# A Mamba layer in rounds: eight states scaled by ScalarE and folded by one accumulating transfer, softplus in one transfer fewer, the output's last passes a round later

## What is computed

```
xv    = silu(conv(x @ W_in) + conv_b)
ssm   = xv @ W_x;  dt_raw, Bp, Cp = split(ssm, (RDT, 16, 16))
delta = softplus(dt_raw @ W_dt + b_dt)
dA    = exp(delta[..., None] * A)
dBx   = delta[..., None] * Bp[:, :, None, :] * xv[..., None]
h     = scan(h -> dA * h + dBx)                  # along the sequence of 512
y     = einsum('bldn,bln->bld', h, Cp) + xv * D  # 16 states n
out   = y @ W_out
```

## Time and profile before

| | |
|---|---|
| median of 3 runs | 754.86 us (753.48 to 755.99) |
| the profiled execution's own time | 754.58 us |
| its span, first to last instruction | 752.7 us |
| busy: PE, DVE, ACT, POOL | 665.7, 645.0, 501.6, 490.3 us |
| mean granted clock of PE | 0.988 |
| from one state-1 add of DVE to that of the next round (549.21 to 602.28) | 53.07 us |

### The profile page before, as it was taken

One profiled execution on the slowest core, in us unless ns is written; L12 is line 12 of the kernel. 1 busy time (PEld: TensorE's weight loads), 2 busy tenths in 40 slices (PEclk: granted clock), 3 DMA queues, 4 the chain that ended last, 5 costly groups with the idle time before them and its releaser, 6 DMA issues. The chain is left out here.

```text
span 752.7 us, 12948 instructions
## 1 busy us (share of the span) xinstructions
PE 665.7 (88%) x4001; PEld 491.8 (65%) x4001; DVE 645.0 (86%) x1102; ACT 501.6 (67%) x1020; POOL 490.3 (65%) x305
## 2 busy tenths in 40 slices
PE   1898999999799998768998998998999999988785
PEld 0885555655565553446876787787777777768765
DVE  5878877777567656989999999999999999999997
ACT  1565666666444444879879778788788797796463
POOL 1001663000055445086999999999999999999995
PEclk9999999999999999989999999999999999999999
DMA  7900110001222217534424336237046156254000
GB/s 203 294 1 7 39 40 28 0 0 28 60 64 68 71 48 98 169 147 127 108 99 128 98 113 144 69 113 182 30 150 151 38 158 154 76 130 120 1 15 16
DMA packets 43050, 67.43 MB, mean 90 GB/s; under 512 B 6264, under 2 KB 30208, under 8 KB 42992
## 3 DMA queue, kind: packets, MB, share of 16 engines
q1 hardware_dynamic: 31744, 48.35, 20.4%
q0 software_dynamic: 9520, 17.78, 11.6%
q10 hardware_dynamic: 1728, 0.57, 0.3%
HBM read 46.01 MB, written 9.67 MB: 74 GB/s over the span
## 5 line engine op out<-in xcount | busy, mean ns | idle before, releaser
L1710 DVE TENSOR_TENSOR_SCAN xnT_all<-psum,nfT_all 128x1024 f32<-128x1024 f32 x128 | 288.5, 2275 | 0.1
L1260 PEld LDWEIGHTS psum<-W_out,xnT_all 128*128 128x128 f32 x2048 | 237.3, 193 | 56.9 <-issue 54.2
L1260 PE MATMUL psum<-W_out,xnT_all 128*128 128x128 f32 x2048 | 242.7, 277 | 29.5 <-DVE acc L1726 27.3
L1433 ACT ACTIVATE psum<-delta,A 128x511 f32<-128x511 f32 x256 | 165.0, 683 | 59.8 <-DVE xnT_all L1710 59.7
L1240 POOL TENSOR_TENSOR nfT_all<-nf_rows,du 128x1024 f32<-128x1024 f32 x63 | 147.2, 2361 | 23.0 <-DVE nfT_all L1792 22.5
L1240 POOL TENSOR_TENSOR nfT_all<-attn_all,du 128x1024 f32<-128x1024 f32 x64 | 157.4, 2601 | 1.1 <-DVE xnT_all L1710 1.1
L571 POOL DMA_INDIRECT moe_dram<-xnT_all x39 | 37.6, 963 | 119.9 <-ACT xnT_all L827 119.9
L1726 DVE SCALAR_TENSOR_TENSOR acc<-psum,Cc,acc 128x128 f32<-128x128 f32 x284 | 77.9, 338 | 6.1 <-PE psum L1260 6.1
L560 POOL DMA_INDIRECT xs_dram<-nf_rows,pos x32 | 33.1, 1036 | 76.3 <-DVE pos L881 57.3
L1260 PE MATMUL psum<-vo_all,W_taps 128*128 128x512 f32 (+3 forms) x128 | 58.7, 606 | 0.7 <-ACT vo_all L1465 0.7
L1484 ACT ACTIVATE ts<-psum,Cc 128x128 f32<-128x128 f32 x188 | 52.8, 360 | 4.1 <-PE psum L1260 4.1
(11 more groups left out here) (218 smaller groups left out, 1128.0 us busy)
## 6 DMA issues: line engine op xcount, KB each, us to landing
nf_rows<-bt_dram SPq DMA_DIRECT2D x32, 512.0 KB, 4.7
attn_all<-bt_dram SPq DMA_DIRECT2D x32, 512.0 KB, 3.9
delta<-rl POOLq DMA_DIRECT2D x7, 512.0 KB, 7.0
e<-ab POOLq DMA_DIRECT2D x7, 512.0 KB, 5.8
delta<-e POOLq DMA_DIRECT2D x7, 512.0 KB, 6.1
xs_dram<-attn_all SPq DMA_DIRECT2D x4, 645.0 KB, 8.3
xnT_all<-xs_dram SPq DMA_DIRECT2D x39, 64.5 KB, 1.9
x_all<-in_x_dram SPq DMA_DIRECT2D x8, 256.0 KB, 6.0
```

The source lines that it names most:

```text
L1260: return nc.tensor.matmul(o, l, r, start=start, stop=stop)
L1433: ins = nc.scalar.activation(dA[:, i % RA, k, 1:L], delta[:, p, h, 1:L], ACT.Exp, scale=A[:, h, 2 * q + k:2 * q + k + 1])
L1710: nc.vector.tensor_tensor_scan(hring[:, i % R, :, :].rearrange("p n l -> p (n l)"), dA[:, i % RA, :, :].rearrange("p n l -> p (n l)"), dbx ...
```

## The change

ACT scales states 8 and 14 as well, so `ON_ACT` has eight states and DVE adds eight. The scaled slices 0 to 3 (states 5, 7, 8, 9) stand in a tile `early`, slices 4 to 7 (11, 12, 14, 15) in `late`, which is a part of `res_all`. Once a round POOL issues one accumulating transfer of 128x2048 values (`fold`) that adds all of `early` onto `late`; three POOL sums then add the four slices of `late`. Two of the softplus transfers become one of 128x2x1024 values (`softplus_sums`, step 6). `output_gate` and `output_rows` of a row move from steps 5 and 7 of the next round to steps 0 and 1 of the round after it, and the store goes with them.

```diff
-        ON_ACT = (5, 7, 9, 11, 12, 15)
+        ON_ACT = (5, 7, 8, 9, 11, 12, 14, 15)
+        FOLD = len(ON_ACT) // 2
+        LAST = sum(n < NS - 2 for n in ON_ACT)
...
-            ts = sb6("ts", [P, len(ON_ACT), TPB, D])
+            early = sb6("early", [P, FOLD, TPB, D])
+            late = res_all[:, 0:FOLD * TPB, :].rearrange("p (i j) d -> p i j d", j=TPB)
...
-                            if end and q == 6:
-                                store()
+                            if b > 1 and q == 2:
+                                store(b - 2)
...
-                    def sum_scaled(c, i):
...
+                    def fold():
+
+                        pool.wait_ge(S["ts"], at(b - 1, "ts", len(ON_ACT)))
+                        alone(pool)
+                        pool.dma_start(late[:, :, :, :], early[:, :, :, :], accum_op=ALU.add).then_inc(s_sp, 16)
+
+                    def sum_folded(i):
+
+                        if i == 1:
+                            pool.wait_ge(s_sp, summed(b, 1))
+                            alone(pool)
+                            pool.wait_ge(S["os"], at(b - 2, "os", 1))
+                        else:
+                            pool.wait_ge(S["accP"], at(b - 1, "accP", i - 1))
+                        nc.gpsimd.tensor_tensor(accP[:, :, :], ts(FOLD) if i == 1 else accP[:, :, :],
+                                                ts(FOLD + i), ALU.add).then_inc(S["accP"], 1)
...
-                    def softplus_high():
+                    def softplus_sums():
                         w("lg", 1)
                         w("rl", KH)
-                        alone(pool)
-                        pool.dma_start(delta[:, 1 - p, :, :], rl[:, :, :], accum_op=ALU.add).then_inc(s_sp, 16)
-
-                    def softplus_low():
                         w("e1", 1)
                         alone(pool)
-                        pool.dma_start(e1[:, :, :], ab[:, :, :], accum_op=ALU.add).then_inc(s_sp, 16)
+                        pool.dma_start(delta_e1[:, 1 - p:3:1 + p, :, :], rl_ab[:, :, :, :], accum_op=ALU.add)\
+                            .then_inc(s_sp, 16)
...
-                            if q in (1, 2, 3) and end:
-                                sum_scaled(b - 1, q + 1)
-                            if q == 4 and end:
-                                sum_scaled(b - 1, 5)
-                                output_sum()
-                            if q == 5:
+                            if q == 0 and b > 1:
+                                output_gate(b - 2)
+                            if q == 1 and b > 1:
+                                output_rows(b - 2)
+                            if q == 3 and end:
+                                fold()
+                            if q == 5 and end:
+                                sum_folded(1)
+                                sum_folded(2)
+                            if q == 6:
                                 if prep:
-                                    softplus_high()
+                                    softplus_sums()
                                 if end:
-                                    output_gate()
-                            if q == 6 and prep:
-                                softplus_low()
+                                    for i in range(3, FOLD):
+                                        sum_folded(i)
                             if q == 7:
-                                if end:
-                                    output_rows()
                                 if prep:
                                     deltas()
-                                sum_scaled(b, 1)
+                                if end:
+                                    output_sum()
...
-                        if q == 0 and end and scan:
-                            scale_state(b - 1, 1 - p, 5)
-                        if scan and 3 <= q < 8:
-                            scale_state(b, p, q - 3)
+                        if scan:
+                            for n in (2 * q - 2, 2 * q - 1):
+                                if n in ON_ACT:
+                                    scale_state(b, p, n)
+                                elif n < 0 and n + NS in ON_ACT and end:
+                                    scale_state(b - 1, 1 - p, n + NS)
```

More of the change, by code:

```diff
@@ L1052, in attention_moe_mamba_ffn @@
             G1 = sb6("G1", [P, 2, L])
[L1053 to L1056, removed]
+            rl_ab = sb6("rl_ab", [P, 2, KH, L])
+            rl, ab = rl_ab[:, 0, :, :], rl_ab[:, 1, :, :]
+            delta_e1 = sb6("delta_e1", [P, 3, KH, L])
+            delta, e1 = delta_e1[:, 0:2, :, :], delta_e1[:, 2, :, :]
             du = sb6("du", [P, 2, KH, L])
@@ L1060, in attention_moe_mamba_ffn, with ts @@
             skip_sb = sb6("skip_sb", [P, 2, TPB, D])
-            ts = sb6("ts", [P, len(ON_ACT), TPB, D])
+            early = sb6("early", [P, FOLD, TPB, D])
+            late = res_all[:, 0:FOLD * TPB, :].rearrange("p (i j) d -> p i j d", j=TPB)
+            def ts(i):
+                return early[:, i, :, :] if i < FOLD else late[:, i - FOLD, :, :]
             accP = sb6("accP", [P, TPB, D])
@@ L1079, in xn1 @@
             def xn1(i):
-                return ts[:, i, :, :] if i < LATER else xnb[:, :, :]
+                return early[:, i, :, :] if i < LATER else xnb[:, :, :]
             names, S = names6, M
@@ L1085, in at, with summed @@
                 return (b + 2) * names[n] + c
+            def summed(b, k):
+                return 16 * (3 * b - (b > 0) + k)
             bM, Gb = (4, 5), (6, 7)
@@ L1120, in round_, with store @@
                             .then_inc(s_bst, 16)
-                    def store():
-                        sp.wait_ge(S["ow"], at(b - 1, "ow", 1))
+                    def store(c):
+                        sp.wait_ge(S["ow"], at(c, "ow", 1))
                         alone(sp)
-                        sp.dma_start(out[ds(b - 1, 1)].rearrange("a (j p) d -> p (a j) d", p=P), ow[:, :, :])\
+                        sp.dma_start(out[ds(c, 1)].rearrange("a (j p) d -> p (a j) d", p=P), ow[:, :, :])\
                             .then_inc(s_o, 16)
@@ L1136, in round_ @@
                                 .then_inc(s_bld[q], 16)
-                            if end and q == 6:
-                                store()
-                    elif end:
-                        store()
+                            if b > 1 and q == 2:
+                                store(b - 2)
+                    elif scan:
+                        store(b - 2)
+                        store(b - 1)
+                    else:
+                        store(b - 1)
                 rounds(sp, round_)
@@ L1203, in drives @@
                     def drives():
-                        pool.wait_ge(s_sp, (b + 1) * 48)
+                        pool.wait_ge(s_sp, summed(b + 1, 0))
                         alone(pool)
@@ L1244, in round_ @@
                             drives()
+                        else:
+                            output_gate(b - 1)
+                            output_rows(b - 1)
                     elif end:
-                        for i in range(2, len(ON_ACT) - 1):
-                            sum_scaled(b - 1, i)
-                        pool.wait_ge(S["accP"], at(b - 1, "accP", len(ON_ACT) - 1))
+                        for i in range(1, LAST):
+                            sum_last(i)
+                        pool.wait_ge(S["accP"], at(b - 1, "accP", LAST - 1))
                         pool.wait_ge(S["G1"], at(b - 1, "G1", 1))
@@ L1427, in decays @@
                     elif q == 0:
-                        act.wait_ge(s_sp, b * 48)
+                        act.wait_ge(s_sp, summed(b, 0))
                     for h in range(KH):
@@ L1475, in conv_silu, with scale_state @@
                         .then_inc(S["yh"], 1)
-                def scale_state(c, p, i):
-                    n = ON_ACT[i]
+                def scale_state(c, p, n):
+                    i = ON_ACT.index(n)
                     act.wait_ge(S["G"], at(c, "G", n + 1))
                     act.wait_ge(S["C"], at(c, "C", 1))
-                    act.wait_ge(S["accP"], at(c, "accP", max(i, 1) + 1 - len(ON_ACT)))
+                    if i >= FOLD:
+                        act.wait_ge(S["accP"], at(c - 1, "accP", max(i - FOLD, 1)))
+                    elif c:
+                        act.wait_ge(s_sp, summed(c, 1))
                     for j in range(TPB):
-                        ins = nc.scalar.activation(ts[:, i, j, :], bank[Gb[n % 2]][:, j * P:(j + 1) * P], ACT.Copy,
+                        ins = nc.scalar.activation(ts(i)[:, j, :], bank[Gb[n % 2]][:, j * P:(j + 1) * P], ACT.Copy,
                                                    scale=Cc[:, p, j, n:n + 1])
```

33 lines of the change are left out of this document (18 added, 15 removed).

## The result

| | before | after |
|---|---|---|
| median of 5 runs each | 755.99 us (753.48 to 757.59) | 767.16 us (761.61 to 767.70) |
| the profiled execution's own time, its span | 754.58, 752.7 us | 761.61, 759.7 us |
| a round, scan (0,0) to scan (0,0), rounds 1 to 5 | 53.07 to 53.08 us | 54.45 us each |

The changed kernel is slower: the ratio is 1.013, with a 95% interval of 1.0093 to 1.0168. The profiled execution is the shortest of its five.

The account below looks back on a forecast made before the run. The prediction took a loop through DVE and PE, 53.07 us a round, as the bound. +8.0 (state 8) + 1.3 (merged transfer) = +9.3 on 754.58 is 763.9; forecast 764.0, 762.5 to 766 at 60%, range 759.5 to 771.

Parts of the forecast that it names:

- State 8: On ACT behind the decays of step 6, it makes PE start state 10 1.33 later; six rounds, +8.0 us.
- DVE's saved adds become waits: DVE saves 1.02 each in steps 5 and 0, but mostly waits longer for PE; 0.25 + 1.02 before state 1.
- no change: Rival: ACT's scaling of state 8 does not hold PE, rounds stay at 53.07; 755.9 us, chance 8%.
- faster: Rival: DVE is the bound by itself, so removed adds of states 8 and 14 give -15.3; 739.3 us, chance 8%.
- State 14: Step 0: DVE's saved 1.02 becomes waiting in rounds 1 to 6; on ACT it costs nothing, by 0.3 us.
- the loop through state 8: DVE's state 1 add through scan (5,1), state 8's removal, then PE until the next state 1 add; 53.07 before.
- The merged transfer: Softplus transfer of doubled size lands after 8.7 (bounds 5.8 and 11.6); free in rounds 1 to 6, +1.3 with round 7.
- The cover of 2 us: In rounds 1 to 6 the merged transfer could land some 2 us later than 8.7 at no cost.
- My second rival: Transfers scale with size: merged one lands after 11.6, deciding from about 10.8; +17, 771.6 us, chance 12%.
- `fold`: Issued by POOL in step 3, lands after 8.5 to 9.7; costs nothing up to some 11.9.
- Round 7: POOL's products bind at scan (1,1), 2.4 later; scan (2,0) 2.2 later, less 0.85 of state 8: +1.3 us.
- the first rival: Merged transfer takes no longer than one before, 5.8 or less: 8.0 - 1.6 = +6.4, 761 us, chance 12%.

Follow-up runs that it names:

- x1: The kernel before with state 8 on ACT in place of state 9, nothing else changed: 763.08 us against 755.54, ratio 1.011.
- x3: The changed kernel with ACT taking state 8 out between the two halves of the decays of step 6, ahead of its wait for scan (5,1): 768.63 us, ratio 1.0189.
- x5: x3 with the softplus sums in two transfers again, the first in step 5: 755.6 us against 754.51, ratio 1.0018.
- x2: The changed kernel with state 10 on ACT instead of state 8: 769.05 us, ratio 1.0172.
- x8: The changed kernel once more, without an edit, for a second profile: 764.23 us against 754.51, ratio 1.0139.
- x6: x3 with fold moving only one slice of four, leaving out the contributions of states 7, 8 and 9: 757.27 us, ratio 1.0037.

## Why the prediction was right, step by step

**State 8: right in place and size.** PE was to start state 10 2.55 behind the scan (5,1) (1.22 + 1.33); it started 2.54 behind it. Rounds 0 to 5 were to become 8.0 longer; they became 1.01 + 5 x 1.375 = 7.9 longer. x1 shows that this part alone does it, and x3 that it is the place in ACT's list and not the work.

**DVE's saved adds become waits: right.** A wait of 1.27 was forecast at the add of state 1; it is 0.52 + 0.66, part of it already at the add of state 0. What DVE wins in step 5 was to lengthen its next wait for PE; ahead of state 13 that grew from 0.62 to 2.43. This and x1 end the rivals "no change" and "faster".

**State 14: right for rounds 1 to 5,** where the loop through state 8 is the whole round; x1, without state 14 on ACT, has the same length.

**The merged transfer: right in effect, 1.0 too long.** It landed after 7.7, not 8.7; the first two rivals needed 5.8 or less and 10.8 or more. Its time on the engines doubled as assumed (2.71 to 5.2). The base was too long: 5.8 was a median, while the very transfer whose 2.71 I used landed after 5.0, and 5.0 + 2.5 is 7.5. The Trainium skill, "DMA: Bandwidth & Descriptors", section "Anatomy of one DMA", would have it at about 4.4 (an estimate by its fit); the trace does not agree, with 7.7 here and 9.5 in x3. Its "Rules for kernel authors" say to coalesce many small transfers into one large one, and call those under 64 KB mostly overhead. The transfers here have 512 KB, and two of them, landing after 5.3 with the first 5.67 ahead, gave shorter rounds than one that the same consumer waits for entirely (x5 against x3).

**The cover of 2 us: held, but is narrower than it reads.** At rounds of 54.45, POOL waits for e1 and for the merged transfer (2.85 and 1.37 in round 4), and from round 1 to round 5 no engine shows a wait for POOL. But this is cover at the pace that state 8 sets. As soon as the loop is shortened, POOL's chain binds (x2, x3) at 53.5 to 56.7. My second rival, transfers of 11.6, had this mechanism and put its threshold at 10.8; in x3 landings of 9.5 sufficed, because the loop no longer gave POOL the time, and `fold` was late as well.

**`fold`: it stayed inside its bound, its neighbours were missed.** It landed after 10.1 (7.7 to 11.4), longer than the 8.5 to 9.7 assumed but inside the bound of 11.9, and POOL waited for it in three of seven rounds (1.4 at most). Its effect on other queues was not in the prediction at all: the loads of B and the store below. No engine shows a wait for these in the trace, so the sum did not suffer.

**Round 7: right in sum, by luck.** Rounds 6 and 7 together became 0.69 + 0.67 = 1.36 longer; +1.3 was forecast. DVE does wait for products, but at the scans (0,0) and (1,0) (1.05 and 1.23), not at (1,1). The merged transfer of round 6 landed after 7.4, and with that the prediction's own reckoning gives about 0: 2.4 less 1.3, 0.23 and 0.85. What made up for it was not foreseen: PE idles for 5.31, until ACT has scaled states 14 and 15 behind late decays, and DVE waits for PE (0.19 and 0.66, before 0.23). PE's clock, of which the prediction says nothing, moves this round by 1.5 between two executions of the changed kernel (last section).

**The sum.** From the first scan of round 0 to the end, the profile after is 9.2 longer than the one before; the forecast was +9.3. That the two agree to 0.1 is luck too: in x8, the same kernel, it is 11.1. The span grew by only 7.0, because that scan stood 2.2 earlier (320.73 against 322.93), in a part of the program that the change does not touch. The median of 767.16 lies 3.2 above the forecast of 764.0, outside the 762.5 to 766 that had 60% but inside the range of 759.5 to 771; 1.1 of the 3.2 comes from the kernel before, whose median is 755.99 beside these runs and was 754.86. x8's median of 764.23 lies 0.2 above it. What the longer of the other runs spend their time on is open: they have no profile, and of the 1.9 us by which the two that exist differ from the first scan on, 1.5 lie in round 7.

**Two slips in the prediction.** 763.9 and 0.3 make 764.2, not 764.0. And the +6.4 beside the estimate for 1 MB is that of the first rival, not the second.

## What to carry to other kernels

When an operation moves from the engine that waits to one that seemed free, ask what stands ahead of it in the new engine's list, since its predecessors' waits come with it: state 8 cost 1.38 us a round though the scaling takes as long on either engine (1.12 on ACT, 1.10 on DVE). Where two engines wait for each other in a loop, a saving pays only on the loop's own path: state 14's add lay outside, and became a wait. And slack on a third engine is measured at the present pace: undoing the change that set the pace can give nothing back, because the next limit stands close behind it (here rounds of 53.5 to 56.7, against 54.45).

## What the runs showed of the hardware that I had not expected

**Transfers beside a large accumulating one.** B's loads landed after 4.7 (median) and the store after 3.9 before:

```profile
nf_rows<-bt_dram SPq DMA_DIRECT2D x32, 512.0 KB, 4.7
...
out_dram<-ow SPq DMA_DIRECT2D x8, 256.0 KB, 3.9
```

After, they go out within 6 us of `fold`, on another queue, and land after 9.9 and 10.1. The same run has the contrast: the five stores beside a `fold` land after 9.6 to 12.8, the three others after 2.3, and B's loads in round 0, which has no `fold`, after 3.6 to 5.6. In x6, with a quarter of the fold, the medians are 5.3 and 7.8. The slowing is mutual: `fold` takes 9.5 to 11.4 in rounds 1 to 6, where B's loads go out beside it, and 7.7 in round 7, where none do. x6's quarter of 256 KB takes 7.4 to 8.9 beside loads and a store, and 3.4 and 4.1 in rounds 1 and 7, without a store. Whether a plain transfer of this size would do the same, no run here shows.

**PE's clock in round 7.** PE idles 5.31 ahead of the projections of states 0 to 3 in the profile after, and 5.51 in x8. Windows (us, busy time and count of PE, PEld, DVE, ACT and POOL, PEclk, DMA share, GB/s) of the idle stretch, the projections and what follows, after:

```profile
700.70:707.80 7.10, 1.83 (x17) 1.64 (x15) 5.85 (x3) 3.76 (x9) 7.10 (x4) 0.97 0.12 37
707.80:714.00 6.20, 6.16 (x42) 6.19 (x43) 5.33 (x10) 3.53 (x8) 6.20 (x5) 0.76 0.01 3
714.00:722.00 8.00, 6.59 (x48) 5.31 (x47) 8.00 (x12) 3.11 (x5) 8.00 (x5) 1.00 0.66 131
```

The projections in x8, the same place before, and a stretch of the same round in x1:

```profile
708.20:715.00 6.80, 6.71 (x34) 6.74 (x35) 4.50 (x6) 3.58 (x8) 6.80 (x5) 0.54 0.01 2
```

```profile
701.00:708.00 7.00, 7.00 (x51) 6.88 (x51) 6.77 (x11) 2.82 (x5) 7.00 (x5) 0.81 0.01 2
```

```profile
700.00:707.00 7.00, 4.33 (x40) 4.17 (x39) 7.00 (x8) 4.20 (x9) 7.00 (x5) 1.00 0.00 0
```

PE's row of these projections after, in x8 and before:

```profile
707.84 8.80 PE L1293 MATMUL psum<-W_out,xnT_all 128*128 128x128 f32 x64 [5.31 <-ACT res_all L1520]
```

```profile
708.29 10.32 PE L1293 MATMUL psum<-W_out,xnT_all 128*128 128x128 f32 x64 [5.51 <-ACT res_all L1520]
```

```profile
699.99 9.21 PE L1260 MATMUL psum<-W_out,xnT_all 128*128 128x128 f32 x64 [2.66 <-DVE acc L1726]
```

A granted clock of 0.54 is nearly all at the lower of the two levels, 1.2 GHz. The 64 matmuls took 8.80 us after and 10.32 in x8. The difference is the 1.5 by which x8's round 7 is longer: DVE's waits for these projections, ahead of the adds of states 0 and 1, are 0.49 and 1.86 there instead of 0.19 and 0.66. In x1, where PE's longest idle stretch there is 2.67, the clock stayed at 1.00 from 700 to 721 us and round 7 took 58.01, the shortest of all. Idle length alone does not decide it: before, the same place shows 0.81 after 2.66. What else does is open.
